# A recurrence run, a one-step gate and a skip term on GpSimd in a gated state-space layer

## The reference, cut to what matters

```python
u = layernorm(x)                                   # 4 x 1024 tokens, 128 features
proj = u @ in_proj_w.T                             # z, xin, B, C, dt, theta, lambda
dt = softplus(dt_raw + dt_bias); lam = sigmoid(lam_raw)
B, C = rope(rms(B) + B_bias), rope(rms(C) + C_bias)  # cos, sin of cumsum(theta), per head
alpha, gamma = exp(-dt * exp(A_log)), lam * dt
beta = (1 - lam) * dt * alpha
for each token:                                    # 32 heads, state 64 x 64
    Bx = outer(x, B)
    h = alpha * h + gamma * Bx + beta * Bx_before
    y = h @ C
y = (y + x * D) * silu(z)
s = (rms(y) * norm_w) @ out_proj_w.T
out = x_in + s * silu(fp8_quantised(u) @ fp8_quantised(ffn_w).T + ffn_b)
```

## Time and profile before

| what | value |
|---|---|
| median of three runs | 1486.18 us (1485.37 to 1486.22) |
| the profiled execution's own time | 1485.21 us |
| its span, first to last instruction | 1483.5 us |
| busy PE / DVE / ACT / POOL | 85% / 89% / 53% / 48% |
| `prepare`, until about | 143 us |
| the units, from the first `hs` to the last | 178.4 to 1402.5 us |
| `finish`, from about | 1418 us |

### The profile page before, as it was taken

The page is one execution under the profiler, slowest core; times in us unless marked ns, Lnnn a source line. Parts: engine busy times, 40 slices in busy tenths (PEclk is TensorE's granted clock), DMA queues, the critical chain, the costliest instruction groups (busy, mean ns, idle before and its releaser), DMA issues. The chain is left out here.

```text
span 1483.5 us, 32371 instructions
## 1 busy us (share of the span) xinstructions
PE 1266.9 (85%) x12252; PEld 922.5 (62%) x12252; DVE 1324.3 (89%) x2280; ACT 790.1 (53%) x1181; POOL 709.0 (48%) x553
## 2 busy tenths in 40 slices
PE   2663599999999999999999999999999999999930
PEld 2552366676666666666666666667676666667620
DVE  7886599998999899989998999899998999899878
ACT  2230366656555556656655555566656556556431
POOL 6000255554555455555555555545555555455514
PEclk9855699999999999999999999999999999999965
DMA  5311442223222332234222422242223222222123
GB/s 162 114 57 39 85 100 58 58 58 73 64 54 61 87 72 58 61 68 91 51 52 46 101 57 58 61 101 58 58 60 74 65 50 61 58 58 58 30 78 92
DMA packets 63447, 101.95 MB, mean 69 GB/s; under 512 B 13547, under 2 KB 27228, under 8 KB 63068
## 3 DMA queue, kind: packets, MB, share of 16 engines
q1 hardware_dynamic: 63292, 99.88, 29.1%
HBM read 23.55 MB, written 9.18 MB: 22 GB/s over the span
## 5 line engine op out<-in xcount | busy, mean ns | idle before, releaser
L1090 POOL TENSOR_TENSOR rot<-part 128x512 f32<-128x512 f32 x256 | 354.5, 1385 | 557.6 <-DVE part L921 535.6
L921 DVE SCALAR_TENSOR_TENSOR part<-bcs,k_prmT,trig 128x512 f32<-128x512 f32 x512 | 453.1, 925 | 0.6 <-DMA trig<-tri 0.4
L939 DVE TENSOR_TENSOR M<-s,E 128x512 f32<-128x512 f32 x256 | 175.6, 686 | 66.1 <-ACT E L1039 63.3
L1039 ACT ACTIVATE E<-d 128x512 f32<-128x512 f32 x256 | 152.9, 597 | 148.5 <-PE d L745 147.8
L1120 POOL TENSOR_TENSOR sqa<-sqa,sq 128x512 f32<-128x512 f32 x112 | 142.1, 1268 | 134.2 <-ACT sq L1044 134.2
L1065 ACT ACTIVATE th<-r 128x512 f32<-128x512 f32 x128 | 76.4, 597 | 209.3 <-PE r L844 209.3
L729 PE MATMUL r<-k_w_zx,xns 128*128 128x256 f32 x512 | 139.0, 394 | 53.4 <-DVE k_carry L958 50.1
L1099 POOL TENSOR_TENSOR ce<-rot,eb 128x512 f32<-128x512 f32 x128 | 159.9, 1271 | 4.2 <-ACT eb L1061 4.2
L763 PEld LDWEIGHTS s<-rot 64*128 64x128 f32 x2048 | 125.1, 188 | 54.9 <-issue 54.1
L763 PE MATMUL s<-rot 64*128 64x128 f32 x2048 | 149.7, 286 | 0.0
L729 PEld LDWEIGHTS r<-k_w_zx,xns 128*128 128x128 f32 x512 | 93.5, 192 | 89.9 <-DVE k_carry L958 68.1
(11 more groups left out here) (233 smaller groups left out, 2096.4 us busy)
## 6 DMA issues: line engine op xcount, KB each, us to landing
trig<-tri SPq DMA_DIRECT2D x512, 128.0 KB, 2.4
bcs<-bc_t SPq DMA_DIRECT2D x16, 256.0 KB, 4.1
bcs<-bc_t SPq DMA_DIRECT2D x32, 128.0 KB, 4.0
a_big<-in_L_attn_u SPq DMA_DIRECT2D x4, 512.0 KB, 6.2
xn_t<-a_xnT SPq DMA_DIRECT2D x1, 2048.0 KB, 7.6
tc_t<-a_tcT SPq DMA_DIRECT2D x1, 2048.0 KB, 12.4
bc_t<-a_tmp SPq DMA_DIRECT2D x1, 2048.0 KB, 7.4
tcs<-tc_t SPq DMA_DIRECT2D x8, 256.0 KB, 3.2
```

Source lines behind the costliest of these rows:

```text
L921: nc.vector.scalar_tensor_tensor(out=part[:, 2 * w + f, :], in0=bcs[:, (t + q // NQ) % 2, 2 * w + f, :], scalar=col, in1=trig[:, p, 1 - f, ...
L939: nc.vector.tensor_tensor(M[:, h, :], Sp[h % 2][:], E[:, h % 2, :], ALU.mult).then_inc(m_ready, 1)
L1039: nc.scalar.activation(E[:, h % 2, :], Dp[:], ACT.Exp).then_inc(e_ready, 1)
L1090: nc.gpsimd.tensor_tensor(rot[:, q % 2, p, w, :], part[:, 2 * w, :], part[:, 2 * w + 1, :], ALU.add).then_inc(rot_ready, 1)
```

## The change

The state recurrence's four steps follow one another on VectorE, and the products that lay between them come after. The gate is one SiLU on ScalarE; the factors 0.5 that the tanh form brought are taken out in `finish` (0.25 / DI becomes 1 / DI, 0.25 becomes 0.5). `xc` is made by GpSimd from `xk`, which lies in SBUF, with the factor `cc` / `kk`: in `prepare` `kk` is kept above 1e-30, and at the start of `units` VectorE takes a reciprocal of `kk` and multiplies `cc` by it. GpSimd's list is reordered.

```diff
+                link(nc.vector.tensor_scalar(K["kk"][:, a:b], K["kk"][:, a:b], TINY, None, ALU.max))
...
                         pe.wait_ge(yt_ready, at(T2, t, 2 * q - 1 + p))
+                        pe.wait_ge(xc_ready, at(T2, t, 2 * q + 2))
...
-                for dst, f in ((xk, "kk"), (xc, "cc")):
...
+                nc.vector.tensor_tensor(xk[:, q % 2, 2 * i:2 * i + 2, :].rearrange("p c (h d) -> p c h d", h=4),
+                                        R[i][:].rearrange("p (c h d) -> p c h d", c=2, h=4),
+                                        bcast(v, [P, 2, 4, HD]), ALU.mult).then_inc(xk_ready, 1)
...
+            nc.vector.reciprocal(inv, K["kk"][:]).then_inc(cc_inverted, 1)
+            dve.wait_ge(cc_inverted, 1)
+            nc.vector.tensor_tensor(K["cc"][:], K["cc"][:], inv, ALU.mult).then_inc(cc_ready, 1)
...
-                    state(t, q, 0)
-                    if live(t, q + 1):
-                        rotation(t, q + 1, 0, 1, 0)
-                    state(t, q, 1)
+                    for c in range(CS):
+                        state(t, q, c)
                     scores(t, q, 2)
-                    state(t, q, 2)
-                    if live(t, q + 1):
-                        rotation(t, q + 1, 0, 1, 1)
-                    state(t, q, 3)
                     if live(t, q + 1):
                         x_scaled(t, q + 1, tn, 0)
+                        rotation(t, q + 1, 0, 1, 0)
                         x_scaled(t, q + 1, tn, 1)
+                        rotation(t, q + 1, 0, 1, 1)
                     scores(t, q, 3)
...
                     for p in range(2):
-                        dve.wait_ge(th_ready, at(T2, t, 2 * q + p + 1))
-                        nc.vector.scalar_tensor_tensor(out=th[:, p, :], in0=th[:, p, :], scalar=1.0, in1=R[p][:],
-                                                       op0=ALU.add, op1=ALU.mult).then_inc(sz_ready, 1)
...
-                        nc.scalar.activation(th[:, p, :], R[p][:], ACT.Tanh, scale=0.5).then_inc(th_ready, 1)
+                        nc.scalar.activation(sz[:, p, :], R[p][:], ACT.Silu).then_inc(sz_ready, 1)
...
+            def x_kept(t, q, tt, i):
+
+                pool.wait_ge(xk_ready, at(T2, t, 2 * q + i + 1))
+                pool.wait_ge(y_ready, at(T2, t, 2 * q - 2))
+                v = K["cc"][:, tt * (CS * H) + 2 * i * H:tt * (CS * H) + 2 * i * H + 2 * H].rearrange("p (c h) -> p c h", h=H)
+                v = v[:, :, 4 * (q % NQ):4 * (q % NQ) + 4].unsqueeze(3)
+                nc.gpsimd.tensor_tensor(xc[:, q % 2, 2 * i:2 * i + 2, :].rearrange("p c (h d) -> p c h d", h=4),
+                                        xk[:, q % 2, 2 * i:2 * i + 2, :].rearrange("p c (h d) -> p c h d", h=4),
+                                        bcast(v, [P, 2, 4, HD]), ALU.mult).then_inc(xc_ready, 1)
...
                     if live(t, q + 1):
-                        sums(t, q + 1, 0)
-                    c_decayed(t, q)
+                        sums(t, q + 1, 0, 0)
+                        x_kept(t, q + 1, tn, 0)
+                    c_decayed(t, q, 0)
                     if live(t, q + 1):
-                        sums(t, q + 1, 1)
+                        x_kept(t, q + 1, tn, 1)
+                        sums(t, q + 1, 0, 1)
+                    c_decayed(t, q, 1)
+                    if live(t, q + 1):
+                        sums(t, q + 1, 1, 0)
+                        sums(t, q + 1, 1, 1)
```

More of the change, by code:

```diff
@@ L45 @@
 MASKED = -1.0e30
+TINY = 1.0e-30
 FP8_MAX = 448.0
@@ L611, in units @@
         rot = sb("rot", [P, 2, 2, 2, ST])
+        inv = rot[:].rearrange("p a b c t -> p (a b c t)")[:, 3 * NC * H:4 * NC * H]
         eb = sb("eb", [P, 2, ST])
@@ L619, in units @@
         hs = sb("hs", [P, CS, 2, HD])
-        th = sb("th", [P, 2, ST])
+        sz = sb("sz", [P, 2, ST])
         yT = sb("yT", [P, 2, ST])
@@ L635, in units @@
         ebs_ready, ce_ready = sem("ebs_ready"), sem("ce_ready")
-        xk_ready, bw_ready = sem("xk_ready"), sem("bw_ready")
-        th_ready, sz_ready, yt_ready, sq_ready = sem("th_ready"), sem("sz_ready"), sem("yt_ready"), sem("sq_ready")
+        xk_ready, xc_ready, bw_ready = sem("xk_ready"), sem("xc_ready"), sem("bw_ready")
+        cc_inverted, cc_ready = sem("cc_inverted"), sem("cc_ready")
+        sz_ready, yt_ready, sq_ready = sem("sz_ready"), sem("yt_ready"), sem("sq_ready")
         sqa_ready = sem("sqa_ready")
@@ L888, in _ @@
         def _(dve):
-            for s in (turned, bw_ready, m_ready, xk_ready, hch, part_ready, sz_ready, yt_ready, mags_done):
+            for s in (turned, bw_ready, m_ready, xk_ready, hch, part_ready, yt_ready, mags_done):
                 dve.sem_inc(s, 1)
@@ L902, in x_scaled @@
                 dve.wait_ge(y_ready, at(T2, t, 2 * q - 2))
-                for dst, f in ((xk, "kk"), (xc, "cc")):
[L904 to L909, removed]
+                v = K["kk"][:, tt * (CS * H) + 2 * i * H:tt * (CS * H) + 2 * i * H + 2 * H].rearrange("p (c h) -> p c h", h=H)
+                v = v[:, :, 4 * (q % NQ):4 * (q % NQ) + 4].unsqueeze(3)
+                nc.vector.tensor_tensor(xk[:, q % 2, 2 * i:2 * i + 2, :].rearrange("p c (h d) -> p c h d", h=4),
+                                        R[i][:].rearrange("p (c h d) -> p c h d", c=2, h=4),
+                                        bcast(v, [P, 2, 4, HD]), ALU.mult).then_inc(xk_ready, 1)
             def rotation(t, q, p, w, f):
@@ L994, in _ @@
                     for p in range(2):
-                        dve.wait_ge(th_ready, at(T2, t, 2 * q + p + 1))
-                        nc.vector.scalar_tensor_tensor(out=th[:, p, :], in0=th[:, p, :], scalar=1.0, in1=R[p][:],
-                                                       op0=ALU.add, op1=ALU.mult).then_inc(sz_ready, 1)
-                    for p in range(2):
                         dve.wait_ge(sz_ready, at(T2, t, 2 * q + p + 1))
@@ L1002, in _ @@
                         dve.wait_ge(sq_ready, at(T2, t, 2 * q))
-                        nc.vector.tensor_tensor(yT[:, p, :], Yp[p][:], th[:, p, :], ALU.mult).then_inc(yt_ready, 1)
+                        nc.vector.tensor_tensor(yT[:, p, :], Yp[p][:], sz[:, p, :], ALU.mult).then_inc(yt_ready, 1)
                     if live(t, q + 1):
@@ L1015, in _ @@
         def _(act):
-            for s in (rounded, sin_ready, absd, e_ready, ebs_ready, th_ready, sq_ready, acc_done, ssq_taken):
+            for s in (rounded, sin_ready, absd, e_ready, ebs_ready, sz_ready, sq_ready, acc_done, ssq_taken):
                 act.sem_inc(s, 1)
@@ L1081, in _ @@
         def _(pool):
-            for s in (rot_ready, ce_ready, sqa_ready):
+            for s in (rot_ready, xc_ready, ce_ready, sqa_ready):
                 pool.sem_inc(s, 1)
-            def sums(t, q, p):
-                for w in range(2):
[L1088 to L1102, removed]
+            def sums(t, q, p, w):
+                pool.wait_ge(part_ready, at(T8, t, 8 * q + 4 * p + 2 * w + 2))
+                pool.wait_ge(y_ready, at(T2, t, 2 * q - 2))
+                nc.gpsimd.tensor_tensor(rot[:, q % 2, p, w, :], part[:, 2 * w, :], part[:, 2 * w + 1, :],
+                                        ALU.add).then_inc(rot_ready, 1)
@@ new lines, in c_decayed @@
+            def c_decayed(t, q, p):
+                pool.wait_ge(ebs_ready, at(T2, t, 2 * q + p + 1))
+                pool.wait_ge(rot_ready, at(T4, t, 4 * q + 4))
+                pool.wait_ge(y_ready, at(T2, t, 2 * q - 1 + p))
+                nc.gpsimd.tensor_tensor(ce[:, p, :], rot[:, q % 2, p, 1, :], eb[:, p, :], ALU.mult).then_inc(ce_ready, 1)
+            def x_kept(t, q, tt, i):
+                pool.wait_ge(xk_ready, at(T2, t, 2 * q + i + 1))
+                pool.wait_ge(y_ready, at(T2, t, 2 * q - 2))
+                v = K["cc"][:, tt * (CS * H) + 2 * i * H:tt * (CS * H) + 2 * i * H + 2 * H].rearrange("p (c h) -> p c h", h=H)
+                v = v[:, :, 4 * (q % NQ):4 * (q % NQ) + 4].unsqueeze(3)
+                nc.gpsimd.tensor_tensor(xc[:, q % 2, 2 * i:2 * i + 2, :].rearrange("p c (h d) -> p c h d", h=4),
+                                        xk[:, q % 2, 2 * i:2 * i + 2, :].rearrange("p c (h d) -> p c h d", h=4),
+                                        bcast(v, [P, 2, 4, HD]), ALU.mult).then_inc(xc_ready, 1)
@@ L1103, in _ @@
+            pool.wait_ge(cc_ready, 1)
+            x_kept(0, 0, 0, 0)
+            x_kept(0, 0, 0, 1)
+            for p in range(2):
+                for w in range(2):
+                    sums(0, 0, p, w)
             for t in range(NS):
@@ L1105, in _ @@
                 for q in range(NQ):
+                    tn = t if q < NQ - 1 else t + 1
                     if live(t, q + 1):
-                        sums(t, q + 1, 0)
-                    c_decayed(t, q)
+                        sums(t, q + 1, 0, 0)
+                        x_kept(t, q + 1, tn, 0)
+                    c_decayed(t, q, 0)
                     if live(t, q + 1):
-                        sums(t, q + 1, 1)
```

(6 more changed lines are left out.)

## The result

| | before | after |
|---|---|---|
| median of four runs | 1486.2 us (1485.37 to 1487.88) | 1601.4 us (1600.19 to 1602.21) |
| ratio, 95% interval | | 1.077 [1.076, 1.079] |
| the profiled execution and its span | 1485.21, 1483.5 us | 1602.21, 1600.3 us |
| busy PE / DVE / ACT / POOL | 85 / 89 / 53 / 48% | 79 / 83 / 49 / 59% |
| first and last `hs` | 178.4, 1402.5 us | 181.5, 1519.4 us |

What follows compares the result with a forecast made beforehand. One unit decides: TensorE is nearly full, and GpSimd's instructions and VectorE's rotations exclude each other. 1485.2 + 110 (63 units at 1.75) + 1 once = 1596 us, SiLU 0; range 1533 to 1653.

Steps and rivals of the forecast that it cites:

- The exclusion: GpSimd's SBUF reads and VectorE's rotations block each other for whole instructions: hold 1.12 us per sum or `ce`, 0.53 per rotation.
- rival (a): No exclusion worth its name for the moved copy, or rotations slip in without delaying GpSimd: -57 us, 1430; chance 0.08.
- The copy's length: GpSimd's skip-term copy with a broadcast factor, in no row: taken as 1.10 us, a hold of 0.95.
- the wait for `k_carry`: TensorE's 0.88 us standstill before x, half 1, until the recurrence's last step; claimed to go.
- The units: Each of the 63 units longer by 1.75 us, 21.0 in all: +110 us.
- The ends of tiles keep their extra: The extra time at tile ends stays as before, so the same 1.75 us applies to all 63 units.
- SiLU: On ScalarE, same durations as tanh, placed behind a 3.17 us wait for z: taken as 0, at most 81 us.
- rival (d): ScalarE becomes late by an exposed table load: 1596 + 81 = 1677 us; chance 0.03.
- Once: One-time cost, taken as +1 us: clamps in `prepare`; reciprocal and product lie in VectorE's wait for the first angles.
- The turning point: Holds from first rotation to last sum take 11.0 us; under 9.3, transposes come before 854.05 and the change gains.
- Rival (b): Partial exclusion: rotations fall into holes, needing another list order; delay 0 to 1 us a unit, 1465 to 1550; chance 0.08.
- The signs: Right: rotations about 1.14 us, units 21.0, VectorE near 80%, GpSimd without holes. Wrong: TensorE's clock off 1.00, a third table load.

Runs made afterwards that it cites:

- e4: The changed kernel with GpSimd's sums, `ce`, copies and squares in the units replaced by fills of about the same length that read nothing; 1432.85 us, 0.964.
- e6: The changed kernel with only GpSimd's list reordered: both `ce` ahead of the second sum, the skip-term copies last; 1473.5 us, 0.992.
- e2: The kernel before with VectorE's order alone: recurrence as a run, then the first M, a rotation behind each half of x; 1734.4 us.
- e8: The kernel of e6 with two of VectorE's rotations moved up, behind the recurrence's first step and ahead of the x scalings; 1451.8 us, 0.977.

## Why the prediction was right, and where it was off

Forecast 1596 us, measured 1601.4. The unit step by step, on the clock of the unit (the times of the traces above less 87.52):

| step | predicted | measured |
|---|---|---|
| M behind the run | 843.30 | 843.32 |
| xk, half 0, starts | 843.90 | 843.92 |
| copy 0 ends | 846.15 | 846.16 |
| `ce` 0 ends | 847.85 | 847.84 |
| copy 1 ends | 849.32 | 849.29 |
| sum of pair 0 ends | 850.97 | 850.96 |
| `ce` 1 ends, Y of pair 1 can start | 852.2 | 852.17 |
| first sum of pair 1 ends | 853.85 | 853.86 |
| last sum ends | 855.73 | 855.76 |
| transposes | 855.80 | 855.82 |

- **The exclusion** was read from three collisions and carried the whole forecast. e4 shows it by itself: without reads on GpSimd, 1433 us, where rival (a), no exclusion, had been priced at 1430. That rival is refuted for the kernel as it is, and its price was right for a kernel whose GpSimd doesn't read.
- **The copy's length**, which no row showed, was taken as 1.10, a hold of 0.95, with bounds of 0.9 and 1.4 for the hold. It is 1.04 where nothing is in its way (e6). In the chain each copy ended 0.91 behind the rotation in its way (932.77 to 933.68), near the 0.95.
- **TensorE**: the wait for `k_carry` went, Y of pair 1 waits 1.67 (predicted 1.8) and the transposes 0.87 (0.9). The clock stayed at 1.00 in the ordinary units, so the sum held; that it might not was named, and e2 shows how much that can cost. In six units that open a tile it did fall.
- **The units** cost 114 us, not 110. An ordinary one is 21.0 us as predicted. "The ends of tiles keep their extra" failed: the first unit of a tile went from 20.6 to 23.4 in five tiles and to 22.8 in two, 18 us in all and not 7 x 1.75 = 12. The other 56, (114 - 18) / 56 = 1.71 each, fell 0.04 short of 1.75, which gives 2 of those 6 us back. Two things make the first units dearer. Before, they had no 0.88 to give back, only a wait of 0.44 (before z); after, they wait 1.79 before Y of pair 1 and 0.86 before the transposes: 2.2 more. And behind the same 1.79 the granted clock fell in five of the seven, which is the difference between 23.4 and 22.8, 3 us in all. One that fell and one that didn't, and the windows from there (columns as in the earlier trace rows):

```profile
364.53 0.68 PE L856 MATMUL y<-k_ident,xc 128*128 128x128 f32 x4 [1.79 <-issue]
1216.71 0.63 PE L856 MATMUL y<-k_ident,xc 128*128 128x128 f32 x4 [1.79 <-issue]
```

```profile
364.50:369.30 4.80, 4.77 (x41) 4.07 (x42) 3.17 (x4) 2.53 (x3) 2.88 (x2) 0.64 0.12 23
1216.70:1221.50 4.80, 3.88 (x45) 3.12 (x46) 3.57 (x5) 2.52 (x3) 2.86 (x2) 1.00 0.12 24
```

- **SiLU** was taken at 0, and its table question fell on the good side: the load stands in the wait for z, two a unit, none added (rival (d) refuted).

```profile
932.55 1.28 ACT L1063 ACT_TABLE_LOAD   x1
934.55 0.60 ACT L1063 ACTIVATE sz<-r 128x512 f32<-128x512 f32 x1 [0.72 <-PE r L848]
```

- **Once** was mis-sized: +3.1 to the first `hs`, not +1. The last `cumT` copy starts at 141.32 for 139.82 behind the clamps, +1.5. The reciprocal did not lie wholly in the wait of the earlier trace rows: it could start only 3.61 after the copies, and with its product it pushed the first angles from 150.90 to 153.34.

```profile
145.61 6.55 DVE L944 RECIPROCAL rot<-k_kk 128x1024 f32<-128x1024 f32 x1 [3.61 <-PEq L59]
152.20 1.22 DVE L946 TENSOR_TENSOR k_cc<-k_cc,rot 128x1024 f32<-128x1024 f32 x1
153.34 0.68 DVE L901 SCALAR_TENSOR_TENSOR ang<-rnd,r 128x512 f32<-128x512 f32 x1
```

So 1485.2 + 113.8 + 3.1 = 1602.1, against 1602.21 of the profiled execution.

- **The turning point** was given as transposes before 854.05. e6 lies on its other side: its last sum ends at 853.69 and the kernel gains 0.8%. Rival (b), rotations in holes by another order, is what e6 and e8 are; it was priced down to 1465, and the best order reached 1452.
- **The parts don't add.** SiLU alone makes -4 us, the run alone +248, the copies alone +161, all three +115. They meet in the same exclusion, the same waits of TensorE and its clock (about 90 of the run's 248), so a part's price depends on the others.
- **The signs** came as named, with three exceptions: VectorE's share is 83%, not near 80; TensorE's clock, whose leaving 1.00 was named as a sign of being wrong, left it in the six units above; and GpSimd's holes in the earlier trace rows were read as 1.3 to 2.7 us, where one of 0.63 stands among them. Of these only the clock moves the sum, by 3 to 4 us.

## What to carry to other kernels

Before work moves from one engine to another, look whether the two share something that both hold for whole instructions; a collision or two in the trace before give the size, and the chain can then be followed to a few hundredths of a microsecond. Count where the moved work lands in the other engine's list, and put what is wanted last where the sharer does something else: the same change lost 115 us with the copies in front and gained 12 with them last and `ce` moved up (the two moves were not tried apart). A wait of TensorE can cost more than its length, and not in every unit alike, so read the granted clock behind each new one in several units.

## What was not expected of the hardware

- TensorE's clock behind a wait: behind 2.59 us without a matmul (e2) the granted clock fell in 54 of 63 units, to between 0.50 and 0.70 over the next 4.8 us, and stayed at 1.00 in nine; behind 1.79 us (the kernel after) it fell in five of seven; behind 1.67 us (the same kernel) in none of 55. So the length of the wait alone doesn't decide it; what else does, no run here takes apart.
- GpSimd's copy with a broadcast factor, reading and writing 128x512 in fp32, takes 1.04 us, less than the 1.27 of a plain sum of two tensors, and a fill of that size 0.53.
- `hs`, a tensor_scalar of 128x128 with a single tensor in SBUF, lasted up to 0.96 us for its free 0.28 while a copy of GpSimd ran (e6), though it has no second tensor in SBUF, only a column of one factor per partition. The Trainium skill (SBUF — State Buffer, Who interferes with whom) lists tensor_scalar among the operations that can take the shared ports in a faster mode; that this one ran in such a mode no run here shows.
